# Stores of two convolutions moved behind their passes, and the sort's keys as 16-bit integers in loads of seven groups

## The chip, the core and the metric

The kernel runs on one NeuronCore of a Trainium2 chip. Its engines work beside each other, each through a queue of its own: TensorE (PE in the profile, its weight loads PEld), VectorE (DVE), ScalarE (ACT), GpSimd (POOL) and SyncE (SP), which here only starts DMAs. The metric is the device time of one execution in microseconds; lower is better. Three executions of the kernel before took 7551.57, 7558.73 and 7559.55 us, median 7558.73.

## The reference

A graph of 6,250 nodes with 128 features and 100,000 edges goes through four graph layers; each layer's output is added to its input and layer-normalized. The first two matter here.

```
x = _layernorm(x + L0(x, edge_weight, W1, b1, W2, b2, Wfc, bfc, edge_index))    # two GCN convolutions, one dense layer
x = _layernorm(x + L1(x, src, dst, ln_gamma, ..., W_ff, b_ff))                  # graph attention
x = _layernorm(x + L2(x, node_type, src, dst, edge_type, ...))                  # heterogeneous attention
x = _layernorm(x + L3(x, edge_index, ...))

_gcn_conv(x, W, b):   h = x @ W;  msg = norm[:, None] * h[src];  agg = segment_sum(msg, dst) + b
norm = dinv[src] * weight * dinv[dst],   dinv = rsqrt(sum of weights into a node)
```

Every convolution thus gathers one row of a table per edge (h[src]), scales it, and adds it up at the edge's destination.

## The kernel before, in words

The program is a chain of stages with a barrier between them (`new_stage`). Nodes are held in 49 tiles of 128 (`NT`). A stage ends when every engine is through its own part of it, SP's waits for its DMAs included.

First stage (L206 to L297): the edges' source, destination, type and weight are loaded as integers (`ld_i`), cast to floats (`ld_f`, L271), transposed by TensorE and copied to `e_in` (L275). The destinations, the sort's keys, are also written to DRAM as 784 rows of 128 floats, `key_d` (L220, L221).

Second stage: a histogram of the nodes. It isn't touched.

Third stage, the sort (L535 to L728): the edges stand in 98 groups of 8 x 128. For each group VectorE builds one-hot rows in bf16 (L334, L587), ranks each edge among equal keys by comparing the edge's key with the keys of its group, which lie replicated in all 128 partitions (`keys_all`; eight `scalar_tensor_tensor` at L613), and works out the row of each edge (L622 to L625). GpSimd then scatters the group's records with eight indirect DMAs (L721), 784 in all. SP loads the replicated keys of a group, 8 x 128 floats to 128 partitions, into one of two buffers as soon as the ranks of the group before the last are done (L542), and once per two groups one tile of the node features (L547), whose number it first loads into a register (`numbers`, L160). The stage's last instructions are a power on GpSimd (L724) and VectorE's product of it.

Fourth stage: the first table, `t0`, x @ W1 scaled, is computed and stored. It isn't touched; its stores (L954) are four to a load of four tile numbers.

Fifth and sixth stage: the two convolutions, `convolve` with `FirstNodes` and `SecondNodes`. The sorted edges stand in 832 columns of 128. GpSimd gathers the rows of a column with one indirect DMA (L757), eight columns to a "half", 104 halves, into four buffers. TensorE multiplies each column by a weighted one-hot matrix (L796), VectorE adds the sums of a half into `acc_gcn` in two additions (L805, semaphore `added`, up to 2 x 104 = 208). Beside that, ScalarE, VectorE and TensorE work on another one-hot product (L1168 to L1236), whose one-hots VectorE makes in bf16 (L915). The last columns are padding, whose source is one and the same row. A pass is also used to work on nodes whose sums are complete: from the sixth turn on one of 45 tiles (`DONE`) per turn, and the last four (`REST`) in a tail behind the pass. In the first convolution that is a bias and a relu in place (L1261, L1267), in the second a chain of ten steps with two layer norms up to the attention's table: features in a row buffer (`feature_rows`, L1472) and scores beside them (`score_rows`, L1477, L1478), 136 floats per node.

SP stores each of those tiles when it is ready: L1299 to `t1` in the first, L1552 to `t2` in the second convolution, and waits for all stores at the end. In the second it then stores another array, `s_loT` (L1560, L1561), made in the same tail. The next pass gathers from the table that was stored. SP's queue holds nothing else in these two stages.

## Time and profile before

| | us |
|---|---|
| median of three executions (lowest, highest) | 7558.73 (7551.57, 7559.55) |
| profiled execution, its own time | 7554.35 |
| its span, first to last instruction | 7552.5 |
| busy in the span: PE, DVE, ACT, POOL | 4910.9, 4682.7, 3188.4, 4883.0 |
| scatters of the sort, first start to last start | 214.6 to 1256.7 |
| gathers of the first pass, first start to last start | 1325.5 to 2390.8 |
| gathers of the second pass, first start to last start | 2417.2 to 3479.8 |

No engine is busy for more than 65% of the span, since the stages have different limits. The profile's instructions stand with their start in us from the span's beginning, their duration, engine, line and operands; the brackets say how long the engine was idle before it and what released it. "issue" is time in which the engine waited for nothing that the profile shows. A DMA's issuing instruction (SPq, or DMA_INDIRECT on POOL) and its transfer are different things: the transfer lands later.

### The profile page before, as it was taken

How to read it: one execution, taken by the hardware profiler on the slowest of the kernel's cores; microseconds unless marked ns; L12 is line 12 of the kernel's file. 1: busy time of each engine (PE TensorE's matmuls, PEld its weight loads, DVE VectorE, ACT ScalarE, POOL GpSimd, SP SyncE). 2: the span in 40 equal slices, each digit the busy share in tenths (PEclk: the TensorE clock that was granted, in tenths of full speed). 3: DMA queues.
4: the chain of work that ended last, by engine and by line, in shares of the span. 5: the costliest groups of instructions: out<-in, count | busy, mean ns of one | idle time of the engine just before them, and what ended most of it. 6: DMA issues, size and time to landing. Idle time of an engine off the chain costs nothing. (4 is left out here: it accounts for less than half of the span.)

```text
span 7552.5 us, 95692 instructions
## 1 busy us (share of the span) xinstructions
PE 4910.9 (65%) x26906; PEld 3728.8 (49%) x26906; DVE 4682.7 (62%) x12437; ACT 3188.4 (42%) x7393; POOL 4883.0 (65%) x4968
## 2 busy tenths in 40 slices
PE   8999801666676777774365655856656666777774
PEld 6777601444444455553254544435555543555553
DVE  8999801555554577775456666645666566566666
ACT  0222200444443444442244444746665642555553
POOL 0677775777776777774777773047777700777774
PEclk9776655888887888886566666967887787899997
DMA  1333201222223222223666665567777822766665
GB/s 29 79 82 79 58 2 28 52 55 55 56 55 48 53 56 55 56 55 56 168 180 183 183 183 118 195 196 230 231 230 224 221 69 82 217 209 210 209 208 146
DMA packets 817681, 925.24 MB, mean 123 GB/s; under 512 B 120147, under 2 KB 656219, under 8 KB 816923
## 3 DMA queue, kind: packets, MB, share of 16 engines
q0 software_dynamic: 198144, 441.54, 23.4%
q1 hardware_dynamic: 395118, 365.43, 16.2%
q10 hardware_dynamic: 223916, 112.15, 5.1%
q8 instruction: 245, 4.01, 0.2%
q14 instruction: 258, 2.11, 0.1%
HBM read 724.85 MB, written 193.87 MB: 122 GB/s over the span
## 5 line engine op out<-in xcount | busy, mean ns | idle before, releaser
L757 POOL DMA_INDIRECT arena<-t,d_src x2496 | 2441.0, 978 | 902.6 <-issue 759.2
L796 PE MATMUL ps<-arena 128*128 128x128 f32 (+2 forms) x8320 | 1779.4, 374 | 755.9 <-DMA arena<-t,d_src 623.5
L796 PEld LDWEIGHTS ps<-arena 128*128 128x128 f32 x8320 | 1567.2, 255 | 1015.7 <-issue 921.6
L805 DVE TENSOR_TENSOR arena<-arena,ps 128x512 f32 (+2 forms) x1040 | 835.4, 803 | 710.4 <-PE ps L796 656.9
L757 POOL DMA_INDIRECT arena<-t,d_typed x832 | 817.2, 982 | 488.8 <-issue 252.7
L721 POOL DMA_INDIRECT d_rec<-arena x784 | 789.0, 1006 | 442.7 <-issue 251.9
L2750 POOL DMA_INDIRECT arena<-t,s_dst x832 | 795.5, 956 | 295.6 <-issue 250.7
L793 PE MATMUL ps<-int_tmp 128*128 128x512 bf16 (+1 forms) x1664 | 554.7, 402 | 475.0 <-DVE arena L805 238.9
L1234 PE MATMUL ps<-arena 128*128 128x416 f16 x3328 | 770.4, 385 | 0.0
L1975 PE MATMUL ps<-arena 128*128 x2496 | 408.5, 296 | 451.7 <-ACT arena L1870 294.2
L1173 ACT ACTIVATE arena<-arena 128x128 f16<-128x128 f16 x1664 | 662.6, 480 | 6.9
L1975 PEld LDWEIGHTS ps<-arena 128*128 128x128 f32 (+1 forms) x2496 | 352.4, 204 | 518.9 <-issue 493.3
L1875 ACT ACTIVATE arena<-iota_row,d_lw 128x128 f32<-128x128 f32 x1664 | 506.5, 387 | 211.6 <-DMA arena<-t,d_src 167.6
L1193 DVE TENSOR_SCALAR arena<-iota_row,d_lw 128x128 f32<-128x128 f32 x1664 | 473.2, 360 | 79.4 <-DVE x_cur L1425 31.9
L1234 PEld LDWEIGHTS ps<-arena 128*128 128x128 f16 x3328 | 334.8, 114 | 249.7 <-issue 103.0
L1168 ACT ACTIVATE arena<-iota_row,arena 128x128 f16<-128x128 f32 x832 | 264.5, 391 | 426.3 <-PE ps L1236 409.5
L793 PEld LDWEIGHTS ps<-int_tmp 128*128 128x128 bf16 x1664 | 154.4, 110 | 581.6 <-DVE arena L805 308.8
L2779 ACT ACTIVATE arena<-iota_row,s_lo 128x128 f32<-128x128 f32 x832 | 254.4, 388 | 430.3 <-PE ps L796 430.3
L2836 DVE TENSOR_TENSOR ps<-ps,arena 128x512 f32<-128x512 f32 x208 | 145.3, 699 | 423.8 <-DMA arena<-t,s_dst 369.8
L2222 DVE TENSOR_TENSOR arena<-ps,arena 128x512 f32<-128x512 f32 x208 | 135.2, 687 | 404.0 <-DMA arena<-t,d_typed 357.6
L1202 DVE TENSOR_SCALAR arena<-arena 128x832 f16<-128x832 f16 x832 | 316.8, 442 | 0.0
L683 PEld LDWEIGHTS ps<-arena 128*128 128x128 f32 x1568 | 258.8, 254 | 53.1 <-issue 45.3
(451 smaller groups left out, 8054.2 us busy)
## 6 DMA issues: line engine op xcount, KB each, us to landing
spill<-arena ACTq DMA_DIRECT2D x208, 512.0 KB, 4.2
arena<-spill SPq DMA_DIRECT2D x208, 512.0 KB, 5.1
arena<-d_loT SPq DMA_DIRECT2D x208, 256.0 KB, 5.0
arena<-s_loT SPq DMA_DIRECT2D x104, 512.0 KB, 4.9
arena<-key_d SPq DMA_DIRECT2D x98, 512.0 KB
t<-arena SPq DMA_DIRECT2D x49, 1024.0 KB, 4.4
arena<-t,d_src POOLq DMA_INDIRECT x2496
arena<-t,d_typed POOLq DMA_INDIRECT x832
```

Of the source, the lines that this page charges most:

```text
L721: pool.indirect_dma_start(out=d_rec[:, :], out_offset=bass.IndirectOffsetOnAxis(ap=row[:, c:c + 1], axis=0), in_=d_recs[:, c, :], in_offse ...
L757: pool.indirect_dma_start(out=rows[r][:, i, :], out_offset=None, in_=table, in_offset=bass.IndirectOffsetOnAxis(ap=idx[:, 8 * n + i:8 * n ...
L793: nc.tensor.matmul(half[:, :, 0:self.width], zeros16[:, 0:P], self.blank, start=True, stop=False, skip_group_check=True)
L796: return nc.tensor.matmul(self.banks[i // 4][:, bass.ds(self.slot[i], self.width)], weights, rows, start=False, stop=False, skip_group_che ...
L805: nc.vector.tensor_tensor(at, at, got, ALU.add).then_inc(self.added, 1)
L1173: last = nc.scalar.activation(at_r[:, b, a, j], far[:, b, j], ACT.Relu, bias=places[:, 2 + 2 * a, at_c + j:at_c + j + 1], scale=places[:, ...
L1193: one_hot = nc.vector.tensor_scalar(at[:, s, :], iota_row[:, :], lw[:, 8 * n + i, 0:1], lw[:, 8 * n + i, 1:2], ALU.is_equal, ALU.mult)
L1202: nc.vector.tensor_scalar(at_q[:, b, j], iota_q, places[:, 0, at_c + j:at_c + j + 1], None, ALU.is_equal)
L1234: nc.tensor.matmul(place_bank(a, z), at_r[:, b, a, j], at_q[:, b, j, z * Q_W:(z + 1) * Q_W], start=False, stop=False, skip_group_check=True)
L1875: last = nc.scalar.activation(at[:, b, i], iota_row[:, :], ACT.Abs, bias=lw[:, 8 * n + i, 0:1], scale=-1.0)
L1975: last = nc.tensor.matmul(looked_up(b, z)[:, (i - 4 * z) * tab_w:(i - 4 * z + 1) * tab_w], hot_T[:, b, i * P:(i + 1) * P], source[:, bass. ...
L2750: pool.indirect_dma_start(out=rows[:, 8 * b + i, :], out_offset=None, in_=t4, in_offset=bass.IndirectOffsetOnAxis(ap=s_dst[:, 8 * n + i:8 ...
```

## The change

In the first stage VectorE also casts the destinations to 16-bit integers (`keys16`), and these are written to `key_d`, now of type int16. In the sort SP loads the keys of seven groups with one DMA (14,336 bytes to each of the 128 partitions), 14 loads instead of 98, into one of two buffers; two loads are issued at the stage's start, then the 48 loads of feature tiles one behind the other, then the other 12 loads of keys, each when the ranks of the seven groups before the last load are done. In both convolutions SP first waits for 204 of the 208 additions, and only then begins to store the 45 tiles. In the second convolution the features no longer go through a row buffer of four tiles: they are written over the tile's sums in `acc_gcn` and the scores to an array for all tiles, so that each tile is stored with two DMAs (128 and 8 floats per node), and VectorE no longer waits for stores.

```diff
-        key_d = dram("key_d", [UG, 8 * EC])
+        key_d = dram("key_d", [UG, 8 * EC], I16)
...
-                sp.wait_ge(edge_f, 1)
+                sp.wait_ge(edge_f, 2)
...
-                sp.dma_start(key_rows[0:full * P, :].rearrange("(j p) e -> p j e", p=P), ld_f[:, 1, 0:full, :]).then_inc(keys_out, 16)
+                sp.dma_start(key_rows[0:full * P, :].rearrange("(j p) e -> p j e", p=P), keys16[:, 0:full, :]).then_inc(keys_out, 16)
...
                 nc.vector.tensor_copy(ld_f[:, 0:3], ld_i).then_inc(edge_f, 1)
+                nc.vector.tensor_copy(keys16, ld_i[:, 1]).then_inc(edge_f, 1)
...
-        keys_all = part(2 * 8 * EC).rearrange("p (b c) -> p b c", b=2)
+        KG = 7
+        keys_all = part(2 * KG * 8 * EC // 2, I16).rearrange("p (b g c) -> p b g c", b=2, g=KG)
...
                 def keys(k):
-                    for b in range(2):
-                        n = 2 * k + b
-                        need(sp, ranked, n - 1)
-                        sp.dma_start(keys_all[:, b, :], key_d[bass.ds(n, 1), :].to_broadcast([P, 8 * EC])).then_inc(keys_in[b], 16)
-
-                def body(k):
-                    keys(k)
+                    need(sp, ranked, KG * (k - 1))
+                    sp.dma_start(keys_all[:, k % 2].rearrange("p g c -> p (g c)"), key_batches[k:k + 1, :].to_broadcast([P, KG * 8 * EC])).then_inc(keys_in[k % 2], 16)
+                key_batches = key_d.rearrange("(k g) c -> k (g c)", g=KG)
+                keys(0)
+                keys(1)
+                for k in range(NT - 1):
                     number, = numbers(sp, k, 1, NT - 2)
                     sp.dma_start(x_cur[:, bass.ds(D * k, D)], t["x"][bass.ds(P * number, P), :]).then_inc(x_in, 16)
-                assert TURNS == NT
-                turns(sp, NT - 1, body)
-                keys(NT - 1)
+                for k in range(2, UG // KG):
+                    keys(k)
...
-                    dve.wait_ge(keys_in[b], 16 * k + 16)
+                    if n % KG == 0:
+                        dve.wait_ge(keys_in[n // KG % 2], 16 * (n // KG // 2) + 16)
...
-                        last = nc.vector.scalar_tensor_tensor(same[:, i], keys_all[:, b, i * EC:(i + 1) * EC], e_in["dst"][:, 8 * n + i:8 * n + i + 1],
+                        last = nc.vector.scalar_tensor_tensor(same[:, i], keys_all[:, n // KG % 2, n % KG, i * EC:(i + 1) * EC], e_in["dst"][:, 8 * n + i:8 * n + i + 1],
...
                     sp.dma_start(t1[bass.ds(P * number, P), :], of_tiles(acc_gcn, t)).then_inc(self.stored, 16)
+                sp.wait_ge(self.sums.added, 2 * HALVES - 4)
                 for t in range(0, DONE):
...
-                need(dve, self.stored, 16 * t)
-                step(nc.vector.tensor_tensor(self.rows[:, 0:w, 0:D], tiled(self.vectors_bank(1, w)), bcast_mid(bias["L1_gnn_b_in"], w), ALU.add))
+                step(nc.vector.tensor_tensor(tiled(of_tiles(acc_gcn, t, w)), tiled(self.vectors_bank(1, w)), bcast_mid(bias["L1_gnn_b_in"], w), ALU.add))
...
-                step(nc.vector.tensor_tensor(self.rows[:, 0:w, D:D + H], uv[:, :, 0:H], bcast_mid(b_u[:, :], w), ALU.add))
+                step(nc.vector.tensor_tensor(tiled(of_tiles(self.scores, t, w, H), H), uv[:, :, 0:H], bcast_mid(b_u[:, :], w), ALU.add))
...
-                def store(t, i):
+                def store(t):
                     number, = numbers(sp, t, 1)
-                    sp.dma_start(t2[bass.ds(P * number, P), :], self.rows[:, i, :]).then_inc(self.stored, 16)
+                    sp.dma_start(t2[bass.ds(P * number, P), 0:D], of_tiles(acc_gcn, t)).then_inc(self.stored, 16)
+                    sp.dma_start(t2[bass.ds(P * number, P), D:D + H], of_tiles(self.scores, t, 1, H)).then_inc(self.stored, 16)
+                sp.wait_ge(self.sums.added, 2 * HALVES - 4)
                 for t in range(0, DONE):
                     sp.wait_ge(self.rows_rdy, 2 * t + 2)
-                    store(t, 0)
+                    store(t)
                 sp.wait_ge(self.rows_rdy, 2 * DONE + 2)
-                for i in range(REST):
-                    store(DONE + i, i)
+                for t in range(DONE, NT):
+                    store(t)
```

SP's queue at the start of the sort, before the change; `arena<-key_d` is a load of keys, `x_cur<-in_x` one of a feature tile, the number of columns stands behind it:

```order
L542 DMA arena<-key_d 128x1024 x2
L160 TENSOR_LOAD s_tile
L547 ISA
L547 DMA x_cur<-in_x 128x128
L542 DMA arena<-key_d 128x1024 x2
L160 TENSOR_LOAD s_tile
L547 ISA
L547 DMA x_cur<-in_x 128x128
```

and with it:

```order
L545 DMA arena<-key_d 128x7168 x2
L160 TENSOR_LOAD s_tile
L551 ISA
L551 DMA x_cur<-in_x 128x128
L160 TENSOR_LOAD s_tile
L551 ISA
L551 DMA x_cur<-in_x 128x128
```

The two first key loads carry seven groups each, and all feature loads stand ahead of the third.

SP's queue in the second convolution, where the stores of a tile begin, before the change; `t<-arena` is a store to the table:

```order
L160 TENSOR_LOAD s_tile
L1552 ISA
L1552 DMA t<-arena 128x136
L160 TENSOR_LOAD s_tile
L1552 ISA
L1552 DMA t<-arena 128x136
```

and with it:

```order
L160 TENSOR_LOAD s_tile
L1557 ISA
L1557 DMA t<-arena 128x128
L1558 ISA
L1558 DMA t<-arena 128x8
```

One store of 136 columns became two, of 128 and 8; in the first convolution the rows of SP's queue are the same before and after, and only the wait ahead of them is new.

## Rows read from the trace of the kernel before

**Rows 1.** Table of groups: line, engine, tiles, count | busy us, mean ns | idle before, releasers.

```profile
L757 POOL DMA_INDIRECT arena<-t,d_src x2496 | 2441.0, 978 | 902.6 <-issue 759.2 <-POOLq L101 142.8 <-DVE arena L2217 0.6
```

**Rows 2.** Line L721, 216 to 902 us, then 920 to 1256: ns least/median/most, starts; idle us, times.

```profile
L721 POOL DMA_INDIRECT d_rec<-arena x507: 963/967/1577, 216.1 to 901.9; - x169
  issue: 164.8, 500
...
L721 POOL DMA_INDIRECT d_rec<-arena x263: 963/967/1304, 919.1 to 1255.4; - x132
  issue: 83.1, 263
```

**Rows 3.** The same view of line L757, 1330 to 2390 us.

```profile
L757 POOL DMA_INDIRECT arena<-t,d_src x829: 944/947/1597, 1330.0 to 2389.5; - x166
```

**Rows 4.** Order of time, first stage: start us, us, engine, line, operation, idle before.

```profile
17.01 0.97 DVE L275 COPY arena<-ps 128x784 f32<-128x784 f32 x1 [1.91 <-PE ps L291]
```

**Rows 5.** Order of time in the sort, a scatter on VectorE's bf16 products.

```profile
408.32 0.76 DVE L587 TENSOR_TENSOR arena<-arena 128x1176 bf16<-128x1176 bf16 x1
408.40 1.51 POOL L721 DMA_INDIRECT d_rec<-arena  x1 [0.30 <-issue]
```

**Rows 6.** Order of time in the sort, a scatter beside none of them.

```profile
740.16 0.97 POOL L721 DMA_INDIRECT d_rec<-arena  x1 [0.30 <-issue]
```

**Rows 7.** DMA queues from 740.1 to 741.2 us: packets, MB, share of 16 engines.

```profile
q1 hardware_dynamic: 66, 0.20, 50.4%
```

**Rows 8.** Order of time in the sort, the scatter behind a pause.

```profile
369.95 0.97 POOL L721 DMA_INDIRECT d_rec<-arena  x1 [4.44 <-issue]
```

**Rows 9.** Order of time, start of the sort.

```profile
200.24 0.82 SPq L542 DMA_DIRECT2D arena<-key_d  x2
...
204.31 0.35 DVE L613 SCALAR_TENSOR_TENSOR arena<-arena,ps 128x128 bf16<-128x128 f32 x1 [1.34 <-DMA arena<-key_d]
```

**Rows 10.** Stretches there: us, PE, PEld, DVE, ACT, POOL busy, PEclk, DMA share, GB/s.

```profile
201.20:203.20 2.00, 2.00 (x13) 1.60 (x12) 1.77 (x4) 0.69 (x1) 0.00 (x0) 0.50 0.84 250
203.20:204.60 1.40, 1.40 (x11) 1.02 (x10) 0.29 (x3) 1.03 (x1) 0.00 (x0) 0.79 0.98 388
```

**Rows 11.** Order of time, end of the first pass.

```profile
2380.90 0.69 DVE L805 TENSOR_TENSOR arena<-arena,ps 128x512 f32 x1 [0.42 <-PE ps L796]
...
2403.57 2.07 PE L796 MATMUL ps<-arena 128*128 128x128 f32 x8 [5.70 <-DMA arena<-t,d_src]
...
2411.64 2.79 SPq L1299 DMA_DIRECT2D t<-arena  x4
```

**Rows 12.** Order of time, SP, 1286.2 to 1288.3 us: stores without a number load between them.

```profile
1286.23 2.01 SPq L954 DMA_DIRECT2D t<-arena  x4
```

**Rows 13.** Stretches in the middle and at the end of the first pass.

```profile
2300.00:2340.00 40.00, 28.56 (x152) 19.82 (x152) 22.35 (x66) 17.70 (x49) 30.25 (x33) 0.83 0.20 54
2365.00:2403.00 38.00, 22.30 (x113) 16.38 (x111) 15.04 (x44) 8.92 (x24) 20.31 (x22) 0.77 0.89 40
```

**Rows 14.** DMA queues from 3474.8 to 3482.6 us, then from 3482.6 to 3483.7.

```profile
q0 software_dynamic: 151, 0.32, 90.7%
t<-arena SPq DMA_DIRECT2D x1, 68.0 KB
...
q1 hardware_dynamic: 143, 0.07, 21.1%
```

**Rows 15.** Order of time, end of the second pass and its tail.

```profile
3470.42 0.69 DVE L805 TENSOR_TENSOR arena<-arena,ps 128x512 f32 x1 [0.42 <-PE ps L796]
...
3522.80 0.29 DVE L1472 TENSOR_TENSOR arena<-ps,bias_sb 128x128 f32<-128x128 f32 x1 [1.01 <-DMA t<-arena]
...
3541.04 0.19 DVE L1478 COPY arena<-ps 128x32 f32<-128x32 f32 x1
```

**Rows 16.** Order of time, SP in the stage behind the second pass.

```profile
3566.50 0.50 SPq L1834 DMA_DIRECT2D arena<-in_L_gnn_w_basis_v  x1
3567.04 2.10 SPq L1836 DMA_DIRECT2D arena<-in_L_gnn_w_comp_k  x1
```

More of the change, by code:

```diff
@@ L195, in build @@
         l3_raw = arena[:, o + 4 * 7 * EC:o + 4 * 7 * EC + 6 * D]
+        o += 4 * 7 * EC + 6 * D
+        keys16 = arena[:, o:o + 7 * EC // 2].bitcast(I16).rearrange("p (j e) -> p j e", j=7)
         SORT0 = 4 * UC
@@ L217, in _ @@
                 sp.wait_ge(x_in, 16)
-                sp.wait_ge(edge_f, 1)
+                sp.wait_ge(edge_f, 2)
                 key_rows = key_d.rearrange("g (c e) -> (g c) e", e=EC)
-                sp.dma_start(key_rows[0:full * P, :].rearrange("(j p) e -> p j e", p=P), ld_f[:, 1, 0:full, :]).then_inc(keys_out, 16)
-                sp.dma_start(key_rows[full * P:UC, :], ld_f[0:UC - full * P, 1, full, :]).then_inc(keys_out, 16)
+                sp.dma_start(key_rows[0:full * P, :].rearrange("(j p) e -> p j e", p=P), keys16[:, 0:full, :]).then_inc(keys_out, 16)
+                sp.dma_start(key_rows[full * P:UC, :], keys16[0:UC - full * P, full, :]).then_inc(keys_out, 16)
                 sp.wait_ge(keys_out, 32)
@@ L509, in build @@
         at_run = part(2 * GH).rearrange("p (b i l) -> p b i l", b=2, i=8)
-        keys_all = part(2 * 8 * EC).rearrange("p (b c) -> p b c", b=2)
         at_loT = part(2 * 8 * EC).rearrange("p (b c) -> p b c", b=2)
-        same = part(8 * EC // 2, BF16).rearrange("p (i e) -> p i e", i=8)
-        rank, val = (part(16) for _ in range(2))
         row = part(UC).bitcast(I32)
@@ L516, in build @@
         s_val = part(UC)
+        same = part(8 * EC // 2, BF16).rearrange("p (i e) -> p i e", i=8)
+        rank, val = (part(16) for _ in range(2))
+        KG = 7
+        keys_all = part(2 * KG * 8 * EC // 2, I16).rearrange("p (b g c) -> p b g c", b=2, g=KG)
+        assert UG % (2 * KG) == 0
         keys_in = [sem("d_keys_in0"), sem("d_keys_in1")]
@@ L1327, in __init__ @@
                 buf = []
-                for n in [REST * D] * 7 + [REST * (D + H), NT * H] + [REST * 6] * 2 + [REST * 2] * 2 + [REST] * 6:
+                for n in [REST * D] * 7 + [0, NT * H] + [REST * 6] * 2 + [REST * 2] * 2 + [REST] * 6:
                     buf.append(scratch(o, n))
@@ L1331, in __init__ @@
                 assert o <= REP_AT
-                self.A, self.aT, self.hT, self.r, self.z, self.zT, self.xiT, rows, self.v_new = buf[0:9]
-                self.rows = rows.rearrange("p (t f) -> p t f", f=D + H)
+                self.A, self.aT, self.hT, self.r, self.z, self.zT, self.xiT, _, self.v_new = buf[0:9]
+                self.scores = arena[:, AT_ACC + NP:AT_ACC + NP + NT * H]
+                assert AT_ACC + NP + NT * H <= AT_Q
                 self.parts = [a.rearrange("p (t c) -> p t c", c=6) for a in buf[9:11]]
@@ L1562, in sync @@
                 sp.wait_ge(self.d_out, 32)
-                sp.wait_ge(self.stored, 16 * NT)
+                sp.wait_ge(self.stored, 32 * NT)
         dec_a, dec_b, dec_h, dec_i = (arena[:, i * SC:(i + 1) * SC] for i in range(4))
```

## The prediction, made before the change was run

> **What bounds the kernel now.** I read the table of groups first, then the instructions of single lines by stage, then the order of time where a stage begins and ends, because the change touches three stages out of many. GpSimd issues one indirect DMA after another in all of them. A gather of the passes keeps it busy for 978 ns on average, and the idle time before the next one is "issue", about 0.3 us each, with no other releaser of size [rows 1]. In the sort it is the same: from 216 to 902 us, 507 scatters begin at a distance of (901.9 - 216.1) / 506 = 1.355 us, and from 919 to 1255, with VectorE long done, 263 at (1255.4 - 919.1) / 262 = 1.284 us [rows 2]. The first pass has 829 gathers in 1059.5 us, 1.280 us each, against a shortest possible 0.944 + 0.305 = 1.249 [rows 3]. So sort and passes last as long as GpSimd's queue; what an edit saves elsewhere counts only before the first issue, behind the last one, or where it shortens an issue. That is how I take the parts.
>
> **Part 1, first stage: 16-bit keys.** VectorE gets a cast of 896 columns between the cast of 2,688 and the first copy from PSUM. That copy waits 1.91 us for TensorE's transposes today [rows 4], and a cast of a third of the columns is under that. The store of the keys starts about 1 us later and has the rest of the stage to land. Cost 0 (0 to 1).
>
> **Part 2, sort: seven groups per load.** What it could gain is in the 0.07 us between the two distances above, 36 us over 507 scatters. The question is whether the key loads make it. In the order of time the long scatter of each group (1.51 us at 408.40) lies on VectorE's one-hot products in bf16 (L334, L587) [rows 5]. A scatter at 740.16, on no such product, takes its usual 0.97 us [rows 6], though in that very 1.1 us the SP queue's key load takes 50.4% of the 16 DMA engines [rows 7]. So the length belongs to VectorE's 16-bit operations, which stay, and the smaller loads give nothing there. The Trainium skill (DMA: Bandwidth & Descriptors, section SWDGE vs HWDGE vs iDMA) says that GpSimd writes its descriptors into SBUF, out of which VectorE locks it in a 2-port mode; by that rule too the loads would save 0, where the whole distance, if it were the loads', would be 36 us and half of it 18.
>
> What does hang on DMA are a few longer pauses: 4.44 us before the scatter at 369.95 [rows 8]. The idle sums show them: 164.8 us over 500 against 0.305 each leaves 12.3 us in the first stretch (four pauses), 83.1 over 263 leaves 2.9 in the quiet one (two pauses) [rows 2]. With loads around, a pause is thus 3.1 us over the usual 0.3, without them 1.45; four pauses cost 6.5 us more. Half the bytes in rare bursts should return most of it. Bounds: -6.5 (all), and +6 if every pause met a burst; I take -4, as a burst fills a small part of the 50 us between loads.
>
> The start pays. VectorE's first rank waits at 204.31 for the first load of 0.5 MB, issued at 200.24 [rows 9]. That load moved at 250 GB/s, the one behind it at 388 [rows 10]. Now the first load is 128 x 14,336 B = 1.84 MB, at 388 GB/s 4.7 us, at 250 GB/s 7.3 us, against 2.1 us. The first rank, the first row numbers and with them GpSimd's whole queue move back by 2.6 to 5.2 us; I take 3.5, as the fast rate held once the transfer had begun. The 48 feature loads that follow on SP's queue are behind both key loads, and the third key load isn't needed before group 14, so they cost 0. Sum of the sort: +3.5 - 4 = -0.5 us.
>
> **Part 3, first pass: stores behind the pass.** Inside the pass the 45 stores cost GpSimd nothing that the row of the gathers shows (median 947 ns, shortest 944, releaser "issue" alone) [rows 3], and the whole excess over the shortest, 0.031 x 829 = 26 us, would be the most they could give back. VectorE's bf16 one-hots run in this pass as in the sort, and the sort's row put the excess on them; I take 0.
>
> At the end SP now waits for the 204th of 208 additions. That one begins at 2380.90 and takes 0.69 [rows 11], so at 2381.6. The four stores of the end follow each other at (2.79 - 0.33) / 3 = 0.82 us (load of the tile number, address, issue) [rows 11]. 49 of them in a row from about 2382.0 put the last issue at 2382.0 + 48 x 0.82 = 2421.4; today it is at 2411.64 + 3 x 0.82 = 2414.1. That is +7.3 us, on the path, since the next stage waits for the stores. Lower bound: if they ran at the distance of stores without a number load, (2.01 - 0.33) / 3 = 0.56 [rows 12], the last 45th would be out at 2407 and the end unchanged, +0.
>
> The stores fall on a busy place. From 2365 to 2403 the DMA engines are 89% busy for 40 GB/s, where mid-pass it is 20% for 54 GB/s [rows 13]: the last gathers are slow, and the last of them releases TensorE only at 2403.57, after a wait of 5.7 us [rows 11]. A store costs each engine 21.1% of 1.1 us = 0.23 us [rows 14]. If all 27 of the window's stores were served at once, the gathers would land 6 us later, and the last four tiles be ready at 2411.6 + 6 = 2417.6, still before SP gets to them at 2418.5. So this is hidden behind SP.
>
> **Part 4, second pass.** SP starts at 3470.42 + 0.69 = 3471.1 [rows 15]. A tile is now two DMAs: 0.82 + 0.56 = 1.38 us. 45 tiles: until 3533.2, ahead of the last scores at 3541.04 [rows 15], with 8 us to spare. Behind them four tiles instead of four stores: 4 x 0.56 = +2.2 us before the DMAs of L1560. VectorE's wait of 1.01 us for the row buffer (L1472) [rows 15] goes: -1.0. The late gathers are not hidden here, since VectorE's long tail starts from them: between 0 (stores served behind the gathers) and 7 us (31 DMAs x 0.23); I take 2, because the one store issued in such a stretch today was served late: issued at 3474.8, none of its packets ran until 3482.6 [rows 14]. Sum: +3.2 us (0 to +8). The skill's page DMA: Bandwidth & Descriptors (Queues, rings and completion order) has each DMA engine alternate between the queues at packet granularity, which speaks against this change: new stores would be served beside the gathers at once. The row disagrees by those 7.8 us; by the rule alone the term would be nearer 7 than 2.
>
> **The sum.** -0.5 + 7.3 + 3.2 = +10.0 us on the profiled execution's 7554.35 (span 7552.5 and 1.9 around it), 7564.4. The median of the runs shown lies 4.4 above that execution; 7558.73 + 10.0 gives **7569 us**. Own range: 7562 to 7580. What a measurement of this kernel can tell from no change is 0.2%, 15 us, so that this is "same", though slower by its sign.
>
> **Rivals.** *SP is held up (slower).* Issuing can block SP: the fourth load of L1834, of 4 x 128 pieces like the three ahead of it, takes 0.50 us to issue, the first of L1836 behind them 2.10 [rows 16]. So SP is held from some 2,048 pieces on, 16 stores of 128. If the slow gathers let none through, SP stands after 16 stores, at 2382 + 13 = 2395, until about 2404: +9.4 on part 3, 16.7 in place of 7.3; in part 4 16 DMAs are 8 tiles, after which SP stands 11 us: the 45th tile is out at 3544.2, the last at 3544.2 + 4 x 1.38 = 3549.7, against 3541.2 + 4 x 0.82 = 3544.5 today, +5.2. Total -0.5 + 16.7 + 5.2 = +21.4, 7580 us. For it: the 7.8 us of no service. Against it: if one store goes between two gather packets, some 12 are served in the 22 us and the pile stays below. It decides where fewer than 11 of the 27 are served.
>
> *The loads and stores were what slowed GpSimd (faster).* Half of the sort's 36 us and a third of the 26 in each pass back: -(18 + 2 x 8.5) + 10.0 = -25, 7534 us. Against it stand [rows 3, 6, 7]; for it only that loads and VectorE's products coincide in most groups.
>
> *The stores fit (no change).* SP needs 0.56 us for a store, part 3 costs 0: -0.5 + 0 + 3.2 = +2.7, 7561 us. Against it: the 0.82 in [rows 11].
>
> **Chances.** Forecast 0.66 (of it 0.50 same, 0.15 slower, 0.01 faster), SP held up 0.18 (slower), GpSimd freed 0.08 (faster), stores fit 0.08 (0.07 same, 0.01 faster). That gives faster 0.10, same 0.57, slower 0.33. The range is 7550 to 7585: the lower end takes in the third case and a run at the profiled execution's level, the upper the first rival with the worst of the key pauses; the second rival stays out.
>
> **What the profile would show.** First rank at 207 to 209.5 us, scatters still about 1.51 us on the one-hot products; pauses of 2 us rather than 4; gathers at 1.280 us as before; SP's last store of the first pass some 7 us later relative to the last gather; in the second pass the four last tiles 2 us longer. I am wrong if the gathers' distance falls toward 1.249, if SP's issue rows in the first pass's end exceed 0.34 us, or if the last gathers of the second pass land more than 7 us later.

## The result, and the profile of the changed kernel

The changed kernel takes 7564.6 us (median, 7554.5 to 7571.7), the kernel before on the same chip 7551.1 (7547.9 to 7559.6): ratio 1.0017, 95% interval 1.0009 to 1.0025, +13.5 us. The profiled execution has 7563.21 us with a span of 7561.4, against 7554.35 and 7552.5.

First the table of groups of the changed kernel, then its row of SP's DMA queue q1 (packets, MB, share of 16 engines). The scatters of the sort (now L725; 788.5 us in sum, 789.0 before) and the gathers of the passes (L761) are as long as before [rows 1], while SP's queue moves 339.5 MB instead of 365.4, the halved keys.

```profile
L761 POOL DMA_INDIRECT arena<-t,d_src x2496 | 2434.5, 975 | 914.3 <-issue 759.2
L725 POOL DMA_INDIRECT d_rec<-arena x784 | 788.5, 1006 | 444.8 <-issue 249.7
q1 hardware_dynamic: 390078, 339.54, 14.2%
```

The start of the sort in order of time (start, us, engine, line, operation, idle before and its releaser), to be held against [rows 9]:

```profile
201.31 0.82 SPq L545 DMA_DIRECT2D arena<-key_d  x2
202.85 12.29 SPq L551 DMA_DIRECT2D x_cur<-in_x  x15
...
208.28 0.35 DVE L617 SCALAR_TENSOR_TENSOR arena<-arena,ps 128x128 bf16<-128x128 int16 x1 [4.24 <-DMA arena<-key_d]
```

The first rank begins 6.97 us behind the issue of its load, where it was 4.07: VectorE waits 4.24 us for the first load of seven groups. The rank itself is as long with 16-bit keys, 0.35 us. The two stretches behind the first issue, to be held against the 250 and 388 GB/s of [rows 10] (the last two columns are the DMA share and GB/s):

```profile
202.20:205.20 3.00, 3.00 (x21) 2.51 (x20) 1.84 (x4) 1.59 (x2) 0.00 (x0) 0.67 1.04 354
205.20:208.00 2.80, 2.25 (x9) 1.00 (x7) 0.00 (x0) 0.20 (x1) 0.00 (x0) 1.00 0.98 379
```

The end of the first pass, to be held against [rows 11]:

```profile
2382.97 42.34 SPq L1303 DMA_DIRECT2D t<-arena  x49
...
2391.56 0.95 POOL L761 DMA_INDIRECT arena<-t,d_src  x1 [0.30 <-issue]
...
2405.42 2.07 PE L800 MATMUL ps<-arena 128*128 128x128 f32 x8 [6.88 <-DMA arena<-t,d_src]
...
2411.60 1.28 ACT L1271 ACTIVATE arena<-arena,dinv 128x128 f32<-128x128 f32 x4 [22.25 <-DVE arena L1265]
2428.10 0.95 POOL L761 DMA_INDIRECT arena<-t,d_src  x1 [35.59 <-POOLq L101]
```

All 49 stores are now one block of SP, which begins 8.6 us ahead of the pass's last gather and ends 33.8 us behind it. The last nodes are computed at 2412.9; in the kernel before their four stores were all that was left from there. GpSimd's next gather waits for the block. From the last gather of the first pass to the first of the second it is 2428.10 - 2391.56 = 36.5 us, where it was 26.5.

The end of the second pass, to be held against [rows 15]:

```profile
3546.12 0.33 SPq L1557 DMA_DIRECT2D t<-arena  x1
3546.64 0.33 SPq L1558 DMA_DIRECT2D t<-arena  x1
...
3551.44 0.19 DVE L1483 COPY arena<-ps 128x32 f32<-128x32 f32 x1
3552.10 0.33 SPq L1557 DMA_DIRECT2D t<-arena  x1
3552.62 0.33 SPq L1558 DMA_DIRECT2D t<-arena  x1
3553.45 0.33 SPq L1557 DMA_DIRECT2D t<-arena  x1
```

The 45th tile goes out at 3546.64, 4.8 us before the last scores: this block is hidden. A tile costs SP 3553.45 - 3552.10 = 1.35 us at the end instead of 0.82.

By stage, in us between GpSimd's first and last indirect DMA of each (all from the two profiled executions):

| | before | changed |
|---|---|---|
| program's start to first scatter | 214.6 | 218.6 |
| sort, first to last scatter | 1042.1 | 1039.7 |
| to the first gather of pass 1 | 68.8 | 69.1 |
| pass 1 | 1065.2 | 1064.2 |
| between passes 1 and 2 | 26.5 | 36.5 |
| pass 2 | 1062.6 | 1062.6 |
| between passes 2 and 3 | 69.5 | 71.1 |
| pass 3 (nothing changed there) | 1070.1 | 1064.4 |

The touched stages sum to +4.0 - 2.4 + 0.3 - 1.0 + 10.0 + 0 + 1.6 = +12.5; the pair's spans differ by only 8.9, since pass 3 was 5.7 us shorter in this execution and what follows it 2.1 longer. One place carries nearly all of it: the space between passes 1 and 2.

### The profile page after: what moved, and what is told of

The parts are those of the page before. It is cut to its first block and busy times, and to the rows that moved or that the text cites. A ratio compares the mean times of both kernels' runs of the same rounds, so it can differ in the third digit from the quotient of the medians.

```text
span 7561.4 us, 95754 instructions
## 1 busy us (share of the span) xinstructions
PE 4920.3 (65%) x26906; PEld 3743.8 (50%) x26906; DVE 4684.3 (62%) x12438; ACT 3189.0 (42%) x7393; POOL 4876.8 (64%) x4968
## 5 line engine op out<-in xcount | busy, mean ns | idle before, releaser
L761 POOL DMA_INDIRECT arena<-t,d_src x2496 | 2434.5, 975 | 914.3 <-issue 759.2
L800 PE MATMUL ps<-arena 128*128 128x128 f32 (+2 forms) x8320 | 1799.8, 377 | 751.3 <-DMA arena<-t,d_src 622.7
L800 PEld LDWEIGHTS ps<-arena 128*128 128x128 f32 x8320 | 1583.3, 257 | 1015.3 <-issue 918.8
L761 POOL DMA_INDIRECT arena<-t,d_typed x832 | 817.9, 983 | 488.6 <-issue 253.3
L725 POOL DMA_INDIRECT d_rec<-arena x784 | 788.5, 1006 | 444.8 <-issue 249.7
L1238 PE MATMUL ps<-arena 128*128 128x416 f16 x3328 | 751.8, 379 | 0.0
L2843 DVE TENSOR_TENSOR ps<-ps,arena 128x512 f32<-128x512 f32 x208 | 145.2, 698 | 426.2 <-DMA arena<-t,s_dst 365.4
L687 PEld LDWEIGHTS ps<-arena 128*128 128x128 f32 x1568 | 265.5, 259 | 55.7 <-issue 46.2
```

Source lines behind the costliest of these rows:

```text
L725: pool.indirect_dma_start(out=d_rec[:, :], out_offset=bass.IndirectOffsetOnAxis(ap=row[:, c:c + 1], axis=0), in_=d_recs[:, c, :], in_offse ...
L761: pool.indirect_dma_start(out=rows[r][:, i, :], out_offset=None, in_=table, in_offset=bass.IndirectOffsetOnAxis(ap=idx[:, 8 * n + i:8 * n ...
L800: return nc.tensor.matmul(self.banks[i // 4][:, bass.ds(self.slot[i], self.width)], weights, rows, start=False, stop=False, skip_group_che ...
L1238: nc.tensor.matmul(place_bank(a, z), at_r[:, b, a, j], at_q[:, b, j, z * Q_W:(z + 1) * Q_W], start=False, stop=False, skip_group_check=True)
```

## Experiments

Distances in us, each from one profiled execution; those of the last two columns run from the last gather of one pass to the first of the next. Ratios are to the kernel before on the same chip. The kernel before has 1042.1, 26.5 and 69.5 in these columns, the changed one 1039.7, 36.5 and 71.1. The times of before were 8786 us for e1 to e4, 7551 for e1b and e5 to e7, 7570 for e3b, e4b, e8 and e9.

| kernel | ratio (95%) | sort, first to last | pass 1 to 2 | pass 2 to 3 |
|---|---|---|---|---|
| e1, first wait alone | 1.0028 (1.0015 to 1.0040) | 1204.7 | 52.8 | 79.9 |
| e2, no waits | 1.0011 (0.9997 to 1.0026) | 1207.8 | 30.1 | 81.3 |
| e3, sort's part alone | 1.0011 (1.0000 to 1.0023) | 1209.0 | 24.8 | 79.9 |
| e4, second pass's part alone | 1.0017 (1.0002 to 1.0032) | 1201.9 | 23.4 | 87.7 |
| e1b, as e1 | 1.0017 (1.0008 to 1.0026) | 1040.0 | 38.1 | 69.5 |
| e3b, as e3 | 1.0000 (0.9991 to 1.0009) | 1036.9 | 25.6 | 69.4 |
| e4b, as e4 | 1.0001 (0.9992 to 1.0010) | 1040.9 | 26.1 | 71.9 |
| e5, a one-hot twice; one execution | 7571.1 us | 1054.0 | 26.2 | 69.6 |
| e6, key loads twice; one execution | 7563.1 us | 1042.3 | 25.8 | 68.9 |
| e7, padding spread | 0.9937 (0.9923 to 0.9951) | 1035.9 | 15.8 | 58.8 |
| e8, changed, padding spread, no waits | 0.9933 (0.9920 to 0.9947) | 1038.9 | 15.1 | 60.2 |
| e9, changed, padding spread | 0.9959 (0.9945 to 0.9973) | 1039.9 | 29.9 | 64.3 |

**e1 and e1b: the wait of the first convolution alone.**

```
                     sp.dma_start(t1[...], of_tiles(acc_gcn, t)).then_inc(self.stored, 16)
+                sp.wait_ge(self.sums.added, 2 * HALVES - 4)
                 for t in range(0, DONE):
```

> The kernel before with one instruction more: SyncE waits ahead of the first convolution's stores until the adding of its pass is all but done; the sort and the second convolution are as before. The pair of profiled executions shows 26.5 us between the last gather of the first pass and the first of the second before, 36.5 us after, with 49 stores at 0.83 us and a few of 1.2 to 1.6 us. Theory A (the wait turns 49 hidden stores into a queue at the end of the pass, and nothing comes back for it): 36 to 37 us there, the whole kernel 9 to 11 us slower than before, ratio about 1.0013, and the first pass itself as long as before (1065 us, its 830 or so gathers beside the convolution's products at a median near 0.95 us). Theory B (stores inside the pass delay the gathers on GpSimd's queue, as one would expect of two users of the same DMA engines): the pass gets shorter by 3 us or more, so that the kernel is slower by 7 us or less. Theory C (the growth of 10 us at this place in the pair was a variation of the one execution): 33 to 34 us there and 7 us slower, the prediction's figure.

e1 ran where the kernel before takes 8786 us. There the engines beside GpSimd fall behind: in 200 us of the sort (600 to 800) ScalarE waits eight times for something the profile calls "remote", 108.5 us in all and 14.7 at most, and TensorE stands idle 41 times, 37.4 us in all, before its products of L705 with the releaser "issue"; neither is in the same 200 us of before. The mean granted clock is 0.72 instead of 0.77. Why that chip is so is open. Order of time at the end of e1's first pass:

```profile
2706.43 0.95 POOL L757 DMA_INDIRECT arena<-t,d_src  x1 [0.30 <-issue]
...
2714.76 41.63 SPq L1299 DMA_DIRECT2D t<-arena  x49
...
2724.64 1.28 ACT L1267 ACTIVATE arena<-arena,dinv 128x128 f32<-128x128 f32 x4 [5.02 <-DVE arena L1261]
2759.18 0.95 POOL L757 DMA_INDIRECT arena<-t,d_src  x1 [51.81 <-POOLq L101]
```

The block of 49 stores is as long as elsewhere, 41.6 us, but begins 8.3 us behind the last gather, since the adding lags further. The distance is 52.8 us; without the wait it is 24.8, 23.4 and 30.1 there (e3, e4, e2), so the wait costs 23 to 29 us at this place and not 10. The whole kernel is 17.5 us slower (+13 to +35). All three theories of this run had the size wrong there.

> The same kernel as e1 (before, with only the wait ahead of the first convolution's stores), since e1 ran where the kernel before itself takes 8786 us instead of 7551: every engine but GpSimd waits there in steps of about 0.7 us per instruction ('issue'), the adding lags behind the gathers, the wait was met 8.3 us behind the pass's last gather instead of 8.6 us ahead of it, and the distance to the next pass's first gather became 52.8 us against 23 to 25 without the wait. Theory A (the cost is 49 issues at 0.83 us, counted from when the adding is all but done, so it depends on how far the adding lags): where the kernel before takes about 7551 us, the stores begin 8 us ahead of the last gather, 36 to 37 us between the passes, 9 to 11 us slower; where it takes about 8786 us, again 50 to 54 us between the passes and 20 us or more slower. Theory B (the wait's cost at the slower place was something else, such as stores that are slower there): the issues' distance is not 0.83 us.

The same kernel on another chip, 7564.8 us against 7551.0: +13.8 us, with an interval of +6 to +20.

```profile
2380.10 43.54 SPq L1299 DMA_DIRECT2D t<-arena  x49
...
2388.38 0.95 POOL L757 DMA_INDIRECT arena<-t,d_src  x1 [0.30 <-issue]
...
2426.43 0.94 POOL L757 DMA_INDIRECT arena<-t,d_src  x1 [37.10 <-POOLq L101]
```

One added instruction gives what the whole change gives, +13.8 of +13.5. The pass is 1064.1 us long, 1.1 less than before in one execution and as long as the changed kernel's; taking its stores out gave the gathers at most that. Theory A's mechanism holds at both places: the block of issues is 41.3 and 43.2 us long, and its price is what of it stands behind the adding. Its sizes were low on e1b's chip (36 to 37 us and +9 to +11; measured 38.1 and +13.8) and, for the whole kernel, high on e1's (20 or more; measured 17.5).

**e2: the change without its two waits; e3 and e3b: the sort's part alone; e4 and e4b: the second convolution's part alone.**

```
-                sp.wait_ge(self.sums.added, 2 * HALVES - 4)     (e2: both)
```

> The changed kernel without its two waits ahead of the stores: the stores of both convolutions go out inside the passes as before; 16-bit keys, seven groups per DMA, early feature loads, rows in place and two DMAs per tile in the second convolution stay. Theory A (the waits are the loss): 10 us at the first pass's end and about 1 to 2 us at the second's come back, so the time is 7553 to 7556 us on the scale where before is 7551 and the changed kernel 7564.6: start of the sort +3, its pauses -2, tail of the second pass -1. Theory B (without its wait the second convolution's stores, now two per tile and one of them of 128 small pieces of 28 bytes, get in the way of GpSimd's gathers inside the pass): the second pass is 5 us or more longer than 1062.6 us and the kernel stays at 7559 or above. Theory C (16 stores held up SyncE, as in the first of the prediction's rivals): no gain from taking the waits away beyond 5 us.

The interval of -3 to +23 us tells nothing by itself; the stages do. The second pass is 1226.0 us with its small stores inside and 1225.9 (e3) without them, so theory B falls; the 30.1 us between the passes are nearer e3's and e4's 24 than e1's 52.8, so theory C falls too. The changed kernel itself wasn't run on this chip; e8 and e9 below repeat the comparison with and without the waits on one chip. (A node has 8 scores, 32 bytes, not the 28 of this expectation and e8's.)

> The kernel before with the sort's part of the change alone: 16-bit keys (the cast, and stores of half the size), seven groups per DMA, all feature loads at the beginning of the sort. Theory A (two small terms that cancel: the first rank waits 7.0 instead of 4.1 us after the issue of the first key load, and GpSimd's six pauses of the sort get shorter by 2 us): +1 us, within 0.2% and hardly different from before; first scatter 3 to 4 us later after the sort's beginning, sort from first to last scatter 1039 to 1041 us against 1042.1. Theory B (GpSimd is freed of the key loads' packets): the scatters get shorter than their mean of before and the kernel is 4 us or more faster. Theory C (larger loads block GpSimd's own descriptors for longer): the pauses grow, 4 us or more slower.

> As e3 (only the sort's part of the change), where the kernel before takes 7551 us. Theory A (only the first load's 3 us; the six pauses of GpSimd differ from execution to execution by more than the change could move, 11 to 18 us in kernels whose sort loads the same keys): +2 to +4 us. Theory B (pauses shorter by 2 to 4 us by the change): -1 to +2 us. Theory C: faster by more, or slower by more, as loads of 1792 KB are worse or better neighbours than 512 KB.

e3 gave 0 to +20 us at the slower place, e3b -1 us by the medians and 0 +- 7 us by the interval. First scatter at 217.4 us in e3b (before 214.6, e1b and e7 with the old loads 215.7). GpSimd's six pauses in the sort, over 0.7 us each, sum to 14.6. In five executions with the old loads (before, e1b, e4b, e5, e7) they sum to 17.1, 16.9, 16.1, 11.2 and 13.5, in four with the new (changed, e3b, e8, e9) to 15.2, 14.6, 11.1 and 15.2: means of 15.0 and 14.0, with a spread of 6 and 4 in the groups. The saving that was expected of them can't be seen, and one of 1 or 2 us can't be excluded.

> The kernel before with the second convolution's part of the change alone: vectors and scores stay in place instead of in a buffer of four tiles, two DMAs per tile instead of one, and the wait ahead of them. Theory A (45 of 49 tiles are stored while the last four tiles are computed, four tiles come behind at 0.5 us more each, less the 1 us for which VectorE waited on the store of its buffer): 71 us between the second pass's last gather and the sort-free stage behind it against 69.5, so +1 to +2 us for the kernel. Theory B (the gain and the loss in the pair were variation): 0 +- 1 us. Theory C (the 45 tiles' stores aren't done before the last four tiles are ready, as they take longer than 1.38 us each): +5 us or more, with SyncE never waiting for the last scores.

> As e4 (only the second convolution's part of the change), where the kernel before takes 7551 us. Theory A (four tiles' second DMAs 2.1 us, less the wait of 1 us on VectorE): +1 to +2 us, 71 us from the second pass's last gather to the next pass's first. Theory B (nothing): within 0.5 us. With e1b's +13.8 us the three parts should then add up to the changed kernel's +13.5 us plus at most 5; if the sum is well above it, the parts share a cost.

e4b: +2.6 us by the medians, within -6 to +8; 71.9 us between the passes against 69.4 in e3b on the same chip. The parts sum to 13.8 - 1.0 + 2.6 = 15.4 us, the whole is 13.5; each of the four has an interval of some +-7, so that a shared cost of that size would not be seen. In e4, where SP starts 15 us behind the last gather, the 45 tiles are no longer hidden: the 45th goes out 5 us behind the last scores, and the distance is 87.7 against 79.9. That is theory C's event, from another cause.

**e5 and e6: what makes the sort's scatters long.** e5 issues one bf16 one-hot of each group again, e6 each key load again, both into buffers that nobody reads.

```
+                    need(dve, lo_hot, n)                                  (e5)
+                    hots(at_more[:, b], d_lo16, n, P)
+                        sp.dma_start(keys_more[:, b, :], key_d[...])...   (e6)
```

> The kernel before, with one of the three bf16 one-hot operations of VectorE per sort group issued a second time, into a buffer that nobody reads (98 operations of about 0.4 us more). It asks what makes the sort's scatters 1.1 to 1.5 us long beside the usual 0.97. Theory V (VectorE's bf16 operations on SBUF hold GpSimd up, whatever else runs): the scatters' excess over 0.97 us, 42 us in sum before, grows by a quarter or more (10 to 20 us). Theory K (the loads of the keys do it, by their packets): excess as before, 40 to 44 us.

> The kernel before, with each of the sort's 98 key loads issued twice, the first time into a buffer that nobody reads (50 MB written to SBUF more, in 98 DMAs of 512 KB). Theory V: the scatters' excess over 0.97 us stays at 40 to 44 us, and the six pauses of GpSimd of 2 to 5 us change by less than 3 us in all. Theory K (key loads lengthen the scatters or GpSimd's pauses, which is what the change could have saved by halving them): excess or pauses grow by 8 us or more.

The scatters' rows in the table of groups, of e5 and then of e6, and e6's row of SP's queue (365.4 MB before):

```profile
L724 POOL DMA_INDIRECT d_rec<-arena x784 | 807.0, 1029 | 438.0 <-issue 245.6
```

```profile
L723 POOL DMA_INDIRECT d_rec<-arena x784 | 788.3, 1005 | 447.2 <-issue 253.2
q1 hardware_dynamic: 409230, 416.82, 18.3%
```

Before, 784 scatters took 789.0 us. One more bf16 operation per group adds 18.0 us to them and 12 to the sort, whose pauses were 5.9 us shorter in this execution. 51.4 MB more of key loads add nothing to them (788.3). The pauses sum to 18.1 us, 1 more than before and 3 above the mean of the five executions with the old loads, so a small effect there stays possible. The first rank waits 4.17 us, as for the changed kernel's large load, as now two loads stand there. Theory V holds for the scatters and theory K, which asked for 8 us or more, falls. (Over 0.965 us apiece the excess was 32.4 us before, not the expectation's 42, and 50.4 in e5.) The operation that was doubled is bf16 and has two inputs in SBUF (TENSOR_TENSOR); which of the two matters, no run separates.

**e7: the padding records name 832 source rows instead of row 0.**

```
-                nc.vector.memset(fill...[:, :, 1], PAD_KEY).then_inc(fill_set, 1)
                 dve.wait_ge(iota_done, 1)
                 step(nc.vector.tensor_copy(iota_c, iota_ci))
+                for field in (0, 2):
+                    step(nc.vector.tensor_copy(fill...[:, :, field], iota_c[:, 0:JC * 16]))
+                nc.vector.memset(fill...[:, :, 1], PAD_KEY).then_inc(fill_set, 1)
```

> The kernel before, but the padding records of the sorted edge table name 832 different source rows instead of all naming row 0 (their weight stays 0, so the sums are the same). The kernel before shows that the pieces of the last four or five gathers of each pass take 1.3 to 1.6 us instead of 0.24 us, and the landing falls 12 us behind GpSimd's last gather. Theory A (the pieces are slow because the padding all reads one row): landing of the last gather within 3 us of its end instead of 12, so about 10 us less in each of the first two passes and less or as much in the three others: 20 to 45 us faster. Theory B (the last gathers are slow for another reason, such as 16-bit and 32-bit stores nearby or the end of the table): no change. Theory C: with the landing early, what follows is bound by the adding instead, and only 5 to 15 us come back.

7502.5 us against 7551.0: 48.5 us faster. GpSimd's queue q0 (packets, MB, share of 16 engines) from 2300 to 2340 us and from 2385 to 2403 of before, the second with the line of all packets:

```profile
q0 software_dynamic: 1014, 2.06, 19.6%
```

```profile
DMA packets 331, 0.67 MB, mean 37 GB/s; under 512 B 170, under 2 KB 170, under 8 KB 330
q0 software_dynamic: 330, 0.66, 87.6%
```

and of e7 from 2380 to 2391, then the order of time there:

```profile
q0 software_dynamic: 242, 0.47, 15.6%
```

```profile
2387.37 0.95 POOL L759 DMA_INDIRECT arena<-t,d_src  x1 [0.30 <-issue]
...
2389.95 1.67 PE L798 MATMUL ps<-arena 128*128 128x128 f32 x8 [3.03 <-DMA arena<-t,d_src]
...
2403.19 0.94 POOL L759 DMA_INDIRECT arena<-t,d_src  x1 [14.87 <-POOLq L101]
```

About half of these packets are 4 bytes long and take 9 ns; the others, which carry the rows, are of 4,096 bytes, 503, 161 and 115 of them by the MB. Such a packet took 40 x 16 x 19.6% / 503 = 0.25 us in the middle of the pass, 18 x 16 x 87.6% / 161 = 1.57 at its end, and 11 x 16 x 15.6% / 115 = 0.24 at the end with the padding spread. The product of the last gather begins 2.6 us behind the gather's start, where it was 12.8 (2403.57 in [rows 11] against 2390.76). The four distances behind passes 1 to 4 shrink by 10.7, 10.7, 14.0 and 14.1 us, 49.5 in sum: theory A, and a little over its range of 20 to 45.

**e8 and e9: both with the padding spread; e8 without the waits and with the first key load split (one group, then six), e9 the changed kernel as it is.**

> The changed kernel without its two waits ahead of the stores, with the first key load split (one group alone, then the other six), and with the padding records spread over 832 source rows as in e7. Theory A (what the change keeps here costs nothing: 16-bit keys and loads of seven groups 0, the split gives back the 3 us of the first load, rows in place take VectorE's wait of 1 us away, two DMAs per tile hidden inside the pass): as e7 or up to 3 us better, 7499 to 7503 us where before takes 7551. Theory B (small stores of 28 bytes per piece inside the second pass get in the gathers' way, or their issues keep SyncE late at the end): 3 us or more above e7.

> The changed kernel, waits kept, with the padding records spread over 832 source rows. Theory A (the stores behind the wait are SyncE's own time and do not care about the slow last gathers): nothing comes back at the end of the first pass (36 to 38 us between the passes, where e7 has 15.8), 7 to 11 us come back at the end of the second pass, where 45 tiles times 1.36 us now end about as late as the last scores, and 14 us in front of each of the next two passes: 35 to 40 us faster than the changed kernel, about 7526 us, and 20 to 28 us slower than e7. The wait's price then is 21 us at the first pass and not 10. Theory B (the stores' issues are slow because the DMA engines are busy with the slow pieces): they get faster with these gone, and the time comes out below 7516 us.

e8 7518.5 us and e9 7537.6, on one chip: 19.1 us between them. The table's distances give 29.9 - 15.1 = 14.8 at the first pass and 64.3 - 60.2 = 4.1 at the second, 18.9 in sum, which accounts for it. e8 is theory A's: 0.67% of 7551 is 51 us, so 7500, and with the small stores inside the second pass it is 1063.5 us long and the distance behind it 60.2 against e7's 58.8. The expectation of e9 was wrong in one point. It took the wait to end when it did before, but the slow last gathers had been holding up the adding too:

```profile
2376.78 41.05 SPq L1305 DMA_DIRECT2D t<-arena  x49
...
2390.67 0.95 POOL L763 DMA_INDIRECT arena<-t,d_src  x1 [0.30 <-issue]
...
2420.61 0.95 POOL L763 DMA_INDIRECT arena<-t,d_src  x1 [28.99 <-POOLq L101]
```

SP begins 13.9 us ahead of the last gather instead of 8.6, and the distance is 29.9 instead of 36.5: 6.6 of e7's 10.7 us did come back, 5.3 of them by the earlier start. So e9 is 19 us behind e8 and not the 20 to 28 behind e7 of the expectation. The block is 1.3 us shorter without the slow packets (41.1 us; 42.3 in the changed kernel), so theory B, that these are what makes the issues slow, falls but for that 1.3. e8's split cut VectorE's wait for the first load from 4.24 to 1.73 us, but there the load was issued 1.9 us later than in e9, so the first scatter is no earlier (217.8; 217.9 in e9). e8 and e7 are each faster than the kernel before (by 0.67% and 0.63%) and aren't told apart.

## Why the prediction was right, point by point

The forecast was +10 us and "same" with a sign toward slower; measured is +13.5 (+7 to +19). Its base of 7558.7 was the median of three; twelve give 7551.1. The predicted 7569 is only 4.4 above the result because 7.6 of base and -3.5 of change nearly cancel; that is luck. So is part of the sum, in which the pauses' -4 and the too small +7.3 are wrong and part 4's +3.2 too large.

- Part 1, cast and store of keys, 0: the first key load is issued at 201.31 us instead of 200.24, 1.1 of the 4.0 in the first row of the table, but over the executions outside the slow chip it comes at 200.2 to 201.5 with the old keys and at 200.0, 201.0, 201.3 and 203.0 with the new (e3b, e9, changed, e8); a cost of more than the 1 us of the bound isn't shown, nor excluded.
- Part 2, scatters stay: right and now shown by e5 and e6. First load +3.5: 2.9 in the pair (6.97 - 4.07), the mechanism confirmed by e8's shorter wait. Pauses -4: this step failed. It took the pauses' excess to come from the loads, by their place in time; e6 doubled the bytes and was 1 us above before (3 above the mean), and the new loads moved the mean by 0.9 us in a spread of 6. The last two pauses are 1.6 to 2.0 us in all of them; what makes the first four longer in one execution than in another is open.
- Part 3, gathers 0: pass 1 was 1065.2 before, 1064.2 changed, 1064.1 in e1b, and 1063.8 to 1067.8 in the others whatever their stores did. The gathers did not move. End +7.3: the mechanism right, the term undersized. From last gather to SP's last issue it was 2414.10 - 2390.76 = 23.3 before and 2424.99 - 2391.56 = 33.4 changed, +10.1. Most stores follow each other at 0.83, but the 48 distances sum to 42.0 us instead of 39.4, as four of them are 1.17 to 1.60 us, and to 41.3, 43.2 and 40.7 in the blocks of e1, e1b and e9. The four stores of [rows 11] were too few to show it.
- Late gathers hidden behind SP: the last product began 13.9 us behind the last gather instead of 12.8, and the last nodes, computed at 2412.9, were 9.6 us before SP came to the 46th store at 2422.5.
- Part 4, +3.2: 1.6 in the pair, 2.5 in e4b against e3b. Behind the last scores the second stores of four tiles cost +2.1, VectorE's wait is -1.0 (from TensorE's last release by a gather to the last scores 48.0 instead of 49.0 us), late gathers +0.5 instead of 2. The 45 tiles' block took 64.5 us instead of 62 and left 4.8 us to spare instead of 8.
- Rival "SP is held up": its event was there, its price was not. The sign "issue rows above 0.34 us" came true in three rows of the block, 0.98 us at 2396.27, 0.69 at 2402.76 and 1.10 at 2403.94. The row of SP's queue from 2382 to 2402.76:

```profile
q1 hardware_dynamic: 1436, 0.65, 10.8%
```

A store is 144 packets, 128 of data and 16 of 4 bytes. 23 stores were issued by then, so 23 x 144 - 1436 = 1,876 packets were outstanding, near the most of the block (1,887) and not far from the rival's 2,048. In e4b's second pass it came closer. The queue's row from 3478 to 3499.9 us, when 27 DMAs had been issued, and the 28th:

```profile
q1 hardware_dynamic: 1856, 0.48, 9.4%
```

```profile
3499.90 0.77 SPq L1553 DMA_DIRECT2D t<-arena  x1
```

That is 27 x 144 - 1856 = 2,032 outstanding. From 3488 to 3501 us of that pass the four issues that began at 2,004 or more took 0.73 to 1.32 us, the ten that began lower 0.33 to 0.41, and no issue left more than 2,032. So SP is held near 2,048, as the rival said, but for 1 us or so at a time, since the stores are served meanwhile; the rival had put it at 9.4 us in the first pass. Whether the two late rows of the first pass are such holds is open: 1,884 packets went with 1.10 us there, 1,888 with 0.33 in e4b. Nor does every long issue row need a full queue: e9 has one of 0.88 us with 144 outstanding, e1b one of 2.41 with 1,296.

The queue's service is the rest of the matter. The first packet of the block's first store ran at 2389.47, 6.5 us behind its issue. From 2382 to 2389.4 only GpSimd's queue moved, from 2389.4 to 2405 both:

```profile
q0 software_dynamic: 133, 0.28, 84.4%
```

```profile
q0 software_dynamic: 272, 0.52, 78.2%
q1 hardware_dynamic: 1952, 0.89, 19.6%
```

0.89 MB are 13.6 stores of 65.5 KB, of the 25 issued by 2405 (not the prediction's 27). In mid-pass the kernel before has 0.8 to 1.0 us from the issue of a store to its first packet, e9, with its quick last gathers, 1.3, and e1b 8.3. The Trainium skill (DMA: Bandwidth & Descriptors, Queues, rings and completion order) has each DMA engine alternate between the queues packet by packet. The trace disagrees with that for the first 6.5 us, in which the gathers' packets of 1.57 us followed each other with no store between them, and agrees for the stretch behind them, in which packets of both queues ran. What holds the first stores back so long is open.

- Rival "GpSimd freed": falls with e6 and with pass 1's length. Rival "the stores fit" at 0.56 us: falls with the 0.83 us of e1b and all other blocks of the first pass.

What stays open: e1b's distance grew by 11.6 us and the changed kernel's by 10.0, medians by 13.8 and 13.5. The 2 to 3 us between distance and median lie inside the intervals, and no stage of the traces shows them. That the wait is most of the change's cost is shown; how the rest splits between sort and second pass is finer than the intervals.

## What to carry to other kernels

Stores that cost nothing inside a loop cost their issue time once a wait gathers them at its end, less what other work still hides: here the first pass's block of 42 us lengthened the end by 10, and in the second pass the 45 tiles' block was hidden whole. Count the instructions, multiply by the measured distance with its outliers, and start from when the wait is really met; another chip moved that by 17 us against the last gather, the spread padding by 5. Whether a neighbour disturbs a queue can be tested by doubling it as well as by taking it out. And padding that all names one row can cost more than the change under study: look at the time per packet where a loop ends.

## What the runs showed of the hardware that was not expected

- Gathers that read one row 128 times: 1.57 us per packet of 4 KB instead of 0.25, 48.5 us over the kernel (e7).
- Stores issued beside such slow gathers: first packet 6.5 to 8.3 us behind the issue (changed kernel, e1b), 1.3 with the padding spread (e9).
- SP's issues took 0.73 to 1.32 us instead of 0.33 with 2,004 to 2,032 packets outstanding on its queue, and none left more than 2,032 (e4b).
- 98 more of VectorE's bf16 operations of 128 x 1024 lengthen GpSimd's indirect DMAs by 18.0 us, 0.18 us per operation (e5); loads of 51.4 MB beside them by nothing (e6).
- The same kernel took 7551, 7570 and 8786 us on three chips. On the last the gathers' own 0.94 us and the stores' 0.83 us were unchanged, while the other engines' instructions came late; the wait added 23 to 29 us between the passes there, and 10 to 12 on the first. The cause is open.
